# A transformer block on one core: a fifth adding transfer in attention, loads in pieces, scores behind the products

## The chip, the cores and the metric

The kernel runs on one core of a Trainium2 chip. The metric is the device time of one execution in microseconds, as the median of several runs. Its engines work side by side, each through its own queue of instructions: TensorE (PE; its weight loads are shown as PEld), VectorE (DVE), ScalarE (ACT), GpSimd (POOL) and SyncE (SP), which here only issues DMA transfers. GpSimd issues DMA transfers of its own, some of which add what they read to what lies at their destination.

## What is computed

The reference is a transformer block over 4 sequences of 2048 tokens with 512 channels: a layer norm, then attention with 16 heads of 32 channels beside a feed-forward part (two chosen experts), and the sum with the input. The change touches attention alone:

```python
attn = jnp.einsum('bhqd,bhkd->bhqk', q, k) * scale
attn = jax.nn.softmax(attn, axis=-1)
out = jnp.einsum('bhqk,bhkd->bhqd', attn, v)
```

## The kernel before

The program has three stages: `dense_stage` (layer norm, queries, keys, values, experts), `attention_stage` and `output_stage`. Only the middle one is changed. It goes through 16 items (a sequence and four of its heads), two to a turn, and through four groups of 512 queries in each item: 64 groups `g`. Keys and queries are held as high and low parts stacked on 96 partitions (`k_x`, `q_x`), with one more row that subtracts the row's maximum.

**Two passes.** For each group TensorE computes the scores twice. *Units* (64 to a group, `mx_ps`) serve the maxima: VectorE reduces each to `unit_max`, and at the end of a group's units a small transpose and ScalarE turn the maxima into `shift`, which SyncE loads into row 96 of the next group's `q_x`. *Scores* (64 to a group, `st_ps`, keys on the partitions) go to ScalarE, which writes their exponentials to `p_sb`, a ring of seven slots. *Products* multiply the exponentials by the values into `o_ps`.

**The order on TensorE** is written out by hand in `STEPS` (line 653): eight strings, one for each step of a group, in which U is a unit of a later group, S a score, V the 16 instructions of products, T the transpose, and Z the matmuls of a sum. A unit, a sum and the transpose each take the next of four banks `mx_ps` and wait until VectorE has read what was in it; a score takes one of three banks `st_ps`.

**The sums of the exponentials.** GpSimd adds the two slots of each pair of key blocks (`pair`, line 832) into one of four slots `p_pair`, named a, b, c, d in a group; eight pair adds to a group. Four adding transfers (`join`, line 839) gather them: a<-b, a<-c, d<-b, d<-c. After the eighth pair add, a ninth add of GpSimd puts b on a (line 874). TensorE sums over the partitions with a matrix of ones (`sums`, line 1017), in three parts listed in `PARTS` (line 603): the part after two transfers in step 7, the part after four transfers in step 2 of the next group, the part after the ninth add in step 3 of the next group. VectorE gathers the three in `sum_raw`.

**The inverse.** SyncE moves the sums into a compact tile (`spread_sums`), VectorE inverts them in step 5 (`invert`), SyncE stores the inverse to DRAM, waits for that store, and reads it back onto all partitions with four transfers (`spread_inverse`, line 750). GpSimd multiplies with it (`normalise`, line 826), in `group` (line 842) ahead of the eighth pair add. ScalarE copies the products out of `o_ps` (`copy_o`, line 889) once the products are done and the normalising of the group before is.

**SyncE's queue** is in order (`turn`, from line 778). At the start of each group it issues the loads of the next item: in the first group keys of two heads, in the next two groups one head each, in the fourth the values, and with each the three parts of a set of queries; then the sums, the shift, the inverse's store and spread, and the store of the group's result.

Of the kernel before, what the change touches and what calls it, by code (L numbers as in the profile page):

```python
# [15 lines left out]
F32 = mybir.dt.float32  # L16
F32R = mybir.dt.float32r
U32 = mybir.dt.uint32
ALU = mybir.AluOpType
# [5 lines left out]
H, D = 16, 32  # L25
# [4 lines left out]
TOK = 512  # L30
# [3 lines left out]
NQ = B * HQ  # L34
KT = N // P
# [540 lines left out]
def attention_stage(nc, qh_d, ql_d, kh_d, kl_d, v_d, inv_d, o_d):  # L576
# [25 lines left out]
    NA, NJ = NP + 1, 4  # L602
    PARTS = [(2, 0, False, 7), (4, 0, True, 10), (0, NA, False, 11)]
    NS = len(PARTS)
    ctx = ExitStack()
    with ctx:
# [3 lines left out]
        def sem(name):  # L610
# [42 lines left out]
        STEPS = ["USUSUSUVUSSUSUSUS", "USUSUSUVUSSUSUSUS", "USUSUSUVZUSSUSUSUS", "USUSUSUVZUSSUSUSUS",  # L653
                 "USUSUSUVUSSUSUSUS", "USUSUSUVUSSUSUSUS", "USUSUSUVTUSSUSUSUS", "USUSUSUVZUSSUSUSUS"]
# [67 lines left out]
        with nc.Block() as block:  # L722

            @block.sync
            def _(sp):
                def load_keys(it, u, heads):
                    for part, src in enumerate((kh_d, kh_d, kl_d)):
                        sp.dma_start(k_x[u][part * D:(part + 1) * D, heads, :].bitcast(F32),
                                     src[it, heads.start * D:heads.stop * D, :].rearrange("(h d) n -> d h n", d=D)).then_inc(k_ld[u], 16)

                def load_values(it, u):
                    sp.dma_start(v_sb[u][:, :, :], v_d[it, :, :, :]).then_inc(v_ld[u], 16)

                def load_queries(it, qc):
                    for part, src in enumerate((qh_d, ql_d, qh_d)):
                        sp.dma_start(q_x[qc][part * D:(part + 1) * D, :, :].bitcast(F32),
                                     src[it, :, qc * TOK:(qc + 1) * TOK].rearrange("(h d) n -> d h n", d=D)).then_inc(q_ld[qc], 16)
# [11 lines left out]

                def spread_inverse(count):  # L750

                    sp.wait_ge(inv_done, count)
                    sp.dma_start(inv_d.rearrange("h (r n) -> (h r) n", n=QR), inv_t[:, :]).then_inc(inv_st, 16)
                    sp.wait_ge(inv_st, count * 16)
# [18 lines left out]
                load_values(0, 0)  # L773
                load_shift(1, 0)

                def turn(L, first, last):
                    for g in range(G):
                        u, qc = g // QC, g % QC
                        it, more = L * 2 + u, not (last and u == 1)
                        if qc == 0 and more:  # L780

                            sp.wait_ge(pv_done, L * G * KT + g * KT)
                            load_keys(it + 1, 1 - u, slice(0, 2))
                        if qc > 0 and more:

                            sp.wait_ge(st_ready, L * G * SK + g * SK)
                            if qc < 3:
                                load_keys(it + 1, 1 - u, slice(qc + 1, qc + 2))
                            else:
                                load_values(it + 1, 1 - u)  # L790
                            load_queries(it + 1, qc - 1)
                        if qc == 0 and not (first and u == 0):
                            sp.wait_ge(st_ready, L * G * SK + g * SK)
                            load_queries(it, QC - 1)
# [12 lines left out]
                spread_sums(ALL_READS + len(PARTS_AT) - PARTS_IN)  # L807
                spread_inverse(NQ * QC)
# [4 lines left out]
            def _(pool):  # L813
# [28 lines left out]
                def group(at):  # L842
                    a, b, c, d = pair_slots(at)
                    if at > 0:
                        pool.wait_ge(joined, at * NJ * 16)
                    pair(at, 0, a)
                    pool.wait_ge(pair_done, at * NA)
# [16 lines left out]
                    pair(at, 5, c)  # L864
                    pool.wait_ge(sum_done, at * NS + 1)
# [125 lines left out]
            def _(pe):  # L991
# [56 lines left out]
                def turn(L, first, last):  # L1048
                    for g in range(G):
                        u, qc = g // QC, g % QC  # L1050

                        def next_unit(j, i):
# [5 lines left out]
                            if n == 0:  # L1058
# [3 lines left out]
                                if (g + ahead) // QC > 0 or not first:  # L1062
                                    pe.wait_ge(k_ld[nu], (L + (g + ahead) // G + nu) * 144)
# [12 lines left out]
                        def products(j):  # L1076
# [6 lines left out]
                            if j == 1:  # L1083
                                pe.wait_ge(v_ld[u], (L + 1) * 16)
# [223 lines left out]
```

## Time and profile before

| | us |
|---|---|
| median of three runs | 4837.95 (4837.81 to 4843.53) |
| the profiled execution, its own time | 4836.55 |
| its span, first to last instruction | 4834.7 |

| engine | busy us | share of the span | instructions |
|---|---|---|---|
| TensorE | 4691.4 | 97% | 24396 |
| TensorE's weight loads | 2773.0 | 57% | 24396 |
| VectorE | 3170.4 | 66% | 5296 |
| ScalarE | 2398.9 | 50% | 4653 |
| GpSimd | 3223.0 | 67% | 1117 |

The shares are averages over three stages. Attention fills about two thirds of the span, from some 1320 to 4640 us, and there GpSimd is busy for 90% or more. A row of a timeline gives the start, the duration and the instruction; instructions of one kind that follow one another are merged, with their count, and the bracket at the end tells how long the engine was idle before and what ended that. Matmuls are pipelined, so the distance between two starts tells more than a duration. SyncE's rows are the issues of transfers, not the transfers.

### The profile page before, as it was taken

The page shows a single profiled execution, that of the slowest core. Times are in us where ns is not written, and L with a number is a line of the kernel's source. Part 1 is how long each engine was busy: PE and PEld are TensorE (multiplying, and loading weights), DVE is VectorE, ACT ScalarE, POOL GpSimd, SP SyncE. Part 2 cuts the span into 40 slices and gives each one's busy share as a digit, 9 for nine tenths or more (in the row PEclk, how much of TensorE's full clock was granted, in tenths as well). Part 3 has the DMA queues.
Part 4 walks back from the last instruction along what each step waited for, and adds up shares of the span by engine and source line. Part 5 has one row for each costly group of instructions (what it writes and reads, how often), then busy time and mean ns, then how long its engine had stood idle before and what let it go on. Part 6 is the DMA issues. An engine that isn't in the chain of part 4 may idle for free. (4 is left out here: it accounts for less than half of the span.)

```text
span 4834.7 us, 66456 instructions
## 1 busy us (share of the span) xinstructions
PE 4691.4 (97%) x24396; PEld 2773.0 (57%) x24396; DVE 3170.4 (66%) x5296; ACT 2398.9 (50%) x4653; POOL 3223.0 (67%) x1117
## 2 busy tenths in 40 slices
PE   8999999999899999999999999999999999999979
PEld 6887878878654444444444444444444444444447
DVE  4223232333188888888888888888888888888534
ACT  2111121121146666666666666666666666666621
POOL 1121212121249998989989989999899998998920
PEclk9999999999979999999999999999999999999989
DMA  5344343343346655656656566665665656655466
GB/s 172 103 127 122 109 138 102 119 129 111 91 106 130 137 127 125 138 125 137 133 124 139 124 131 136 126 139 120 132 137 124 140 125 132 137 124 121 90 225 236
DMA packets 254215, 633.49 MB, mean 131 GB/s; under 512 B 45252, under 2 KB 79044, under 8 KB 212936
## 3 DMA queue, kind: packets, MB, share of 16 engines
q0 software_dynamic: 36864, 268.45, 27.8%
q1 hardware_dynamic: 217032, 360.85, 27.0%
q8 instruction: 193, 3.16, 0.3%
q14 instruction: 126, 1.03, 0.1%
HBM read 224.96 MB, written 134.74 MB: 74 GB/s over the span
## 5 line engine op out<-in xcount | busy, mean ns | idle before, releaser
L927 DVE TENSOR_REDUCE unit_max<-mx_ps 128x1 f32<-128x512 f32 x4096 | 2535.2, 681 | 317.0 <-PE mx_ps L1002 310.9
L836 POOL TENSOR_TENSOR p_pair<-p_sb 128x2048 f32<-128x2048 f32 x512 | 2439.8, 4811 | 185.3 <-PE mx_ps L1026 128.3
L913 ACT ACTIVATE p_sb<-st_ps 128x512 f32<-128x512 f32 x4096 | 2061.9, 628 | 905.5 <-PE st_ps L1073 905.5
L1002 PE MATMUL mx_ps<-k_x,q_x 96*128 96x512 f32 x4096 | 1684.9, 415 | 21.5 <-DMA k_x<-k_lo_d 19.6
L1073 PE MATMUL st_ps<-q_x,k_x 97*128 97x512 f32 x4096 | 1607.8, 413 | 37.9 <-ACT p_sb L913 37.3
L1073 PEld LDWEIGHTS st_ps<-q_x,k_x 97*128 97x128 f32 x4096 | 770.3, 188 | 599.3 <-ACT p_sb L913 512.8
L1002 PEld LDWEIGHTS mx_ps<-k_x,q_x 96*128 96x128 f32 x4096 | 784.6, 192 | 456.7 <-DVE unit_max L927 234.3
L1014 PE MATMUL o_ps<-p_sb,v_sb 128*32 128x512 f32 x8192 | 986.8, 599 | 0.0
L285 POOL TENSOR_TENSOR h_lo<-h_f,h_hi 128x512 fp32r<-128x512 f32 x128 | 165.2, 1291 | 687.7 <-DVE h_hi L469 687.7
L1014 PEld LDWEIGHTS o_ps<-p_sb,v_sb 128*32 128x32 f32 x8192 | 214.0, 109 | 494.1 <-ACT p_sb L913 309.8
L469 DVE CAST h_hi<-h_f 128x512 fp32r<-128x512 f32 x128 | 55.0, 431 | 541.9 <-ACT h_f L342 541.9
L342 ACT ACTIVATE h_f<-rot,b_sb 128x512 f32<-128x512 f32 x128 | 88.2, 689 | 642.3 <-PE rot L505 642.3
L840 POOL DMA_DIRECT2D p_pair<-p_pair x256 | 244.2, 954 | 159.9 <-DMA p_pair<-p_pair 134.4
L874 POOL TENSOR_TENSOR p_pair<-p_pair 128x2048 f32<-128x2048 f32 x64 | 293.5, 4586 | 5.0
L326 ACT ACTIVATE qk_hi<-rot,qk_bias 128x512 fp32r<-128x512 f32 x128 | 88.2, 689 | 384.2 <-DMA q_lo_d<-qk_lo 176.3
L944 DVE TENSOR_TENSOR sum_raw<-mx_ps,sum_raw 128x512 f32<-128x512 f32 x128 | 88.5, 691 | 207.4 <-PE mx_ps L1026 207.4
L503 PE MATMUL rot<-xnT_hi,wq_hi 128*128 128x512 f32 x512 | 201.8, 394 | 18.1 <-DVE qk_lo L433 9.9
L503 PE MATMUL acc<-we_hi,h_hi 128*128 128x512 f32 x512 | 205.5, 401 | 6.0 <-POOL h_lo L285 4.4
L1026 PE MATMUL mx_ps<-p_pair,ones 128*32 128x512 f32 x1536 | 201.7, 597 | 9.8 <-DMA p_pair<-p_pair 7.8
L268 POOL TENSOR_TENSOR rstd<-var_eps,minus_half 128x4 f32<-128x4 f32 (+1 forms) x17 | 16.9, 992 | 287.4 <-DVE var_eps L372 287.4
L433 DVE SCALAR_TENSOR_TENSOR qk_lo<-rot,qk_bias,qk_hi 128x512 fp32r<-128x512 f32 x128 | 95.7, 748 | 164.8 <-ACT qk_hi L326 164.4
L503 PE MATMUL rot<-xnT_hi,we_hi 128*128 128x512 f32 x512 | 200.0, 391 | 1.9 <-DVE v_out L455 1.9
(94 smaller groups left out, 3926.8 us busy)
## 6 DMA issues: line engine op xcount, KB each, us to landing
p_pair<-p_pair POOLq DMA_DIRECT2D x256, 1024.0 KB, 7.3
q_x<-q_hi_d SPq DMA_DIRECT2D x128, 256.0 KB, 8.6
k_x<-k_hi_d SPq DMA_DIRECT2D x68, 256.0 KB, 7.3
xt<-x SPq DMA_DIRECT2D x64, 256.0 KB, 2.7
stage<-w SPq DMA_DIRECT2D x32, 512.0 KB, 5.1
q_hi_d<-qk_hi SPq DMA_DIRECT2D x64, 256.0 KB, 3.0
q_lo_d<-qk_lo SPq DMA_DIRECT2D x64, 256.0 KB, 3.9
k_hi_d<-qk_hi SPq DMA_DIRECT2D x64, 256.0 KB, 2.6
```

The costliest lines, as they stand in the source:

```text
L285: pool.tensor_tensor(h_lo[:, n % 2, :], h_f[:, n % 2, :], h_hi[:, n % 2, :].bitcast(F32), ALU.subtract).then_inc(h_lo_done, 1)
L433: dve.scalar_tensor_tensor(out=qk_lo[:, m % 2, :], in0=rot[m % 4][:, :], scalar=qk_bias[:, m:m + 1], in1=qk_hi[:, m % 2, :].bitcast(F32), ...
L503: pe.matmul(out, lh, rh, start=start and k == 0, stop=False)
L836: pool.tensor_tensor(p_pair[:, slot, :, :], p_sb[:, n % SLOTS, :, :], p_sb[:, (n + 1) % SLOTS, :, :], ALU.add).then_inc(pair_done, 1)
L840: pool.dma_start(p_pair[:, into, :, :], p_pair[:, slot, :, :], accum_op=ALU.add).then_inc(joined, 16)
L874: pool.tensor_tensor(p_pair[:, a, :, :], p_pair[:, a, :, :], p_pair[:, b, :, :], ALU.add).then_inc(pair_done, 1)
L913: act.activation(p_sb[:, (L * G * KT + n) % SLOTS, h, :], st_ps[bank(g, m)][:, :], ACT.Exp, scale=SCALE).then_inc(exp_done, 1)
L927: dve.reduce_max(unit_max[:, n // 4, n % 4:n % 4 + 1], mx_ps[UNIT_PLACE[n] % RING][:, :], AX.X).then_inc(bank_read, 1)
L1002: pe.matmul(mx_ps[UNIT_PLACE[n] % RING][:, :], q_x[qc][0:R, h, t * P:(t + 1) * P], k_x[u][0:R, h, kc * 512:(kc + 1) * 512], start=True, st ...
L1014: op = pe.matmul(o_ps[rows, :], v_sb[u][:, kt, rows], p_sb[:, (L * G * KT + n) % SLOTS, h, :], start=(kt == 0), stop=(kt == KT - 1))
L1026: op = pe.matmul(mx_ps[place % RING][h * D:(h + 1) * D, :], ones[:, :], p_pair[:, slot, h, :], start=True, stop=True)
L1073: pe.matmul(st_ps[bank(g, m)][:, :], k_x[u][:, h, kt * P:(kt + 1) * P], q_x[qc][:, h, :], start=True, stop=True).then_inc(st_ready, 1)
```

## The change

It does six things in the attention stage.

- The ninth add of GpSimd becomes a fifth adding transfer, a<-b, which waits for the eighth pair add and for the fourth transfer. The last part of the sums now waits for five transfers (`NA`, `NJ`, `PARTS`).
- At the start of a group the first pair add waits for four transfers of the group before, the second one for all five.
- `normalise` moves from behind the fourth transfer to ahead of the wait before the seventh pair add.
- The loads of keys and values are cut into four pieces to a group, of 256 KB each, and those of the queries into three. They wait for scores of the group: two pieces for the 10th, two for the 16th, two query parts for the 33rd, one for the 57th, and stand on SyncE's queue between the other transfers.
- The store of the inverse is issued ahead of the load of the shift instead of behind it.
- In `STEPS`, two scores instead of a unit follow the products (or the sum or transpose behind them), and two units come together later in the step.

GpSimd's order, one group, from its first two pair adds on. Before (L836 is a pair add, L840 a transfer, L830 normalising, L874 the ninth add):

```order
L836 TENSOR_TENSOR p_pair<-p_sb 128x2048 x2
L840 DMA p_pair<-p_pair 128x2048
L836 TENSOR_TENSOR p_pair<-p_sb 128x2048 x2
L840 DMA p_pair<-p_pair 128x2048
L836 TENSOR_TENSOR p_pair<-p_sb 128x2048
L840 DMA p_pair<-p_pair 128x2048
L836 TENSOR_TENSOR p_pair<-p_sb 128x2048 x2
L840 DMA p_pair<-p_pair 128x2048
L830 TENSOR_TENSOR o_inv<-o_raw,o_inv 128x512
L836 TENSOR_TENSOR p_pair<-p_sb 128x2048
L874 TENSOR_TENSOR p_pair<-p_pair 128x2048
```

Now (L855 a pair add, L859 a transfer, L849 normalising):

```order
L855 TENSOR_TENSOR p_pair<-p_sb 128x2048 x2
L859 DMA p_pair<-p_pair 128x2048
L855 TENSOR_TENSOR p_pair<-p_sb 128x2048 x2
L859 DMA p_pair<-p_pair 128x2048
L855 TENSOR_TENSOR p_pair<-p_sb 128x2048
L859 DMA p_pair<-p_pair 128x2048
L855 TENSOR_TENSOR p_pair<-p_sb 128x2048
L849 TENSOR_TENSOR o_inv<-o_raw,o_inv 128x512
L855 TENSOR_TENSOR p_pair<-p_sb 128x2048
L859 DMA p_pair<-p_pair 128x2048
L855 TENSOR_TENSOR p_pair<-p_sb 128x2048
L859 DMA p_pair<-p_pair 128x2048
```

Normalising stands one pair add and one transfer earlier, and the last row is a transfer.

SyncE's order, one group with keys of one head. Before:

```order
L728 DMA k_x<-k_hi_d 32x2048 x2
L728 DMA k_x<-k_lo_d 32x2048
L736 DMA q_x<-q_hi_d 32x4x512
L736 DMA q_x<-q_lo_d 32x4x512
L736 DMA q_x<-q_hi_d 32x4x512
L748 DMA sum_t<-sum_raw 128x1x16
L742 DMA q_x<-shift 1x16x128
L753 DMA inv_d<-inv_t 128x16
L758 DMA o_inv<-inv_d 32x512 x4
L764 DMA o_d<-o_inv 128x512
```

Now, the group with the pieces of two heads:

```order
L727 DMA k_x<-k_lo_d 32x2048
L727 DMA k_x<-k_hi_d 32x2048 x2
L727 DMA k_x<-k_lo_d 32x2048
L752 DMA sum_t<-sum_raw 128x1x16
L736 DMA q_x<-q_hi_d 32x4x512
L736 DMA q_x<-q_lo_d 32x4x512
L756 DMA inv_d<-inv_t 128x16
L746 DMA q_x<-shift 1x16x128
L764 DMA o_inv<-inv_d 32x512 x4
L736 DMA q_x<-q_hi_d 32x4x512
L770 DMA o_d<-o_inv 128x512
```

Four pieces of keys stand ahead of the sums, two parts of the queries behind them, the inverse ahead of the shift, and the last part of the queries behind the spread of the inverse.

TensorE's order around the products of a plain step (mx_ps is a unit, st_ps a score, o_ps the products). Before:

```order
L1014 MATMUL o_ps<-p_sb,v_sb 32x512 x8
L1002 MATMUL mx_ps<-k_x,q_x 128x512
L1073 MATMUL st_ps<-q_x,k_x 128x512 x2
L1002 MATMUL mx_ps<-k_x,q_x 128x512
L1073 MATMUL st_ps<-q_x,k_x 128x512
L1002 MATMUL mx_ps<-k_x,q_x 128x512
L1073 MATMUL st_ps<-q_x,k_x 128x512
L1002 MATMUL mx_ps<-k_x,q_x 128x512
```

Now:

```order
L1035 MATMUL o_ps<-p_sb,v_sb 32x512 x8
L1094 MATMUL st_ps<-q_x,k_x 128x512 x2
L1023 MATMUL mx_ps<-k_x,q_x 128x512
L1094 MATMUL st_ps<-q_x,k_x 128x512
L1023 MATMUL mx_ps<-k_x,q_x 128x512 x2
L1094 MATMUL st_ps<-q_x,k_x 128x512
L1023 MATMUL mx_ps<-k_x,q_x 128x512
L1094 MATMUL st_ps<-q_x,k_x 128x512
```

Behind the products stand two scores where a unit and two scores stood; two units come together three rows later.

The diff, cut to its core:

```diff
-    NA, NJ = NP + 1, 4
-    PARTS = [(2, 0, False, 7), (4, 0, True, 10), (0, NA, False, 11)]
+    NA, NJ = NP, 5
+    PARTS = [(2, 0, False, 7), (4, 0, True, 10), (5, 0, False, 11)]
...
-        STEPS = ["USUSUSUVUSSUSUSUS", "USUSUSUVUSSUSUSUS", "USUSUSUVZUSSUSUSUS", "USUSUSUVZUSSUSUSUS",
-                 "USUSUSUVUSSUSUSUS", "USUSUSUVUSSUSUSUS", "USUSUSUVTUSSUSUSUS", "USUSUSUVZUSSUSUSUS"]
+        STEPS = ["USUSUSUVSSUSUUSUS", "USUSUSUVSSUSUUSUS", "USUSUSUVZSSUSUUSUS", "USUSUSUVZSSUSUUSUS",
+                 "USUSUSUVSSUSUUSUS", "USUSUSUVSSUSUUSUS", "USUSUSUVTSSUSUUSUS", "USUSUSUVZSSUSUUSUS"]
...
-                        if qc == 0 and more:
-
-                            sp.wait_ge(pv_done, L * G * KT + g * KT)
-                            load_keys(it + 1, 1 - u, slice(0, 2))
...
+                        def load(part, score):
+
+                            if part < 4 and more:
+                                sp.wait_ge(st_ready, L * G * SK + g * SK + score)
+                                if qc < 3:
+                                    load_keys(it + 1, 1 - u, (4 * qc + part) // 3, (4 * qc + part) % 3)
+                                else:
+                                    load_values(it + 1, 1 - u, part)
...
+                        load(0, 10)
+                        load(1, 10)
+                        load(2, 16)
+                        load(3, 16)
                         if not (first and g == 0):
                             spread_sums(read_count(L, g, PART_PLACE[LAST_PART], first, last))
+                        load(4, 33)
+                        load(5, 33)
+                        if not (first and g == 0):
+                            store_inverse(L * G + g)
                         if not (last and g == G - 1):
                             load_shift(L * G + g + 2, (qc + 1) % QC)
                         if not (first and g == 0):
                             spread_inverse(L * G + g)
+                        load(6, 57)
+                        if not (first and g == 0):
                             store_group(L, it - 1 if qc == 0 else it, (qc - 1) % QC, L * G + g)
...
                     if at > 0:
+                        pool.wait_ge(joined, (at * NJ - 1) * 16)
+                    pair(at, 0, a)
+                    if at > 0:
                         pool.wait_ge(joined, at * NJ * 16)
-                    pair(at, 0, a)
-                    pool.wait_ge(pair_done, at * NA)
                     pair(at, 1, b)
...
                     pair(at, 5, c)
+                    if at > 0:
+                        normalise(at)
                     pool.wait_ge(sum_done, at * NS + 1)
                     pair(at, 6, a)
                     pool.wait_ge(pair_done, at * NA + 6)
                     pool.wait_ge(joined, (at * NJ + 3) * 16)
                     join(d, c)
-                    if at > 0:
-                        normalise(at)
                     pair(at, 7, b)
                     pool.wait_ge(pair_done, at * NA + NP)
-                    pool.tensor_tensor(p_pair[:, a, :, :], p_pair[:, a, :, :], p_pair[:, b, :, :], ALU.add).then_inc(pair_done, 1)
+                    pool.wait_ge(joined, (at * NJ + 4) * 16)
+                    join(a, b)
```

## Rows read from the trace of the kernel before

**Rows 1.** TensorE's timeline, one group: start, us, line, instruction, count, [idle <-releaser]

```profile
3003.04 1.92 PE L1014 MATMUL o_ps<-p_sb,v_sb 128*32 128x512 f32 x16
...
3008.95 1.92 PE L1014 MATMUL o_ps<-p_sb,v_sb 128*32 128x512 f32 x16
...
3012.00 0.63 PE L1073 MATMUL st_ps<-q_x,k_x 97*128 97x512 f32 x2
...
3013.16 0.43 PE L1073 MATMUL st_ps<-q_x,k_x 97*128 97x512 f32 x1
...
3015.39 0.40 PE L1002 MATMUL mx_ps<-k_x,q_x 96*128 96x512 f32 x1
3015.72 1.92 PE L1014 MATMUL o_ps<-p_sb,v_sb 128*32 128x512 f32 x16
...
3046.97 1.92 PE L1014 MATMUL o_ps<-p_sb,v_sb 128*32 128x512 f32 x16
...
3051.04 0.50 PE L1073 MATMUL st_ps<-q_x,k_x 97*128 97x512 f32 x1 [0.55 <-ACT p_sb L913]
...
3053.65 1.92 PE L1014 MATMUL o_ps<-p_sb,v_sb 128*32 128x512 f32 x16
```

**Rows 2.** Waits, 56 groups: engine, line <- releaser: us in total, times, longest

```profile
ACT o_raw L893 <- POOL o_inv L830: 122.7, 56, 2.5
POOL p_pair L840 <- DMA p_pair<-p_pair: 119.0, 56, 2.7
```

**Rows 3.** GpSimd's timeline, the same group

```profile
3008.35 9.13 POOL L836 TENSOR_TENSOR p_pair<-p_sb 128x2048 f32<-128x2048 f32 x2
3017.78 0.89 POOL L840 DMA_DIRECT2D p_pair<-p_pair  x1 [0.30 <-POOL p_pair L836]
...
3027.50 1.19 POOL L840 DMA_DIRECT2D p_pair<-p_pair  x1
...
3035.27 0.88 POOL L840 DMA_DIRECT2D p_pair<-p_pair  x1 [1.96 <-DMA p_pair<-p_pair]
...
3043.08 4.62 POOL L836 TENSOR_TENSOR p_pair<-p_sb 128x2048 f32<-128x2048 f32 x1 [2.28 <-PE mx_ps L1026]
3047.64 0.86 POOL L840 DMA_DIRECT2D p_pair<-p_pair  x1
3048.26 1.55 POOL L830 TENSOR_TENSOR o_inv<-o_raw,o_inv 128x512 f32<-128x512 f32 x1
3049.49 4.86 POOL L836 TENSOR_TENSOR p_pair<-p_sb 128x2048 f32<-128x2048 f32 x1
3054.43 4.59 POOL L874 TENSOR_TENSOR p_pair<-p_pair 128x2048 f32<-128x2048 f32 x1
```

**Rows 4.** Stretches: us, busy by engine, then PEclk, DMA share, GB/s

```profile
3048.90:3054.10 5.20, 4.65 (x20) 2.63 (x24) 4.26 (x7) 4.20 (x9) 5.20 (x2) 1.00 1.03 202
3108.00:3108.50 0.50, 0.50 (x4) 0.30 (x2) 0.50 (x2) 0.50 (x2) 0.50 (x1) 1.00 1.11 246
3157.50:3158.00 0.50, 0.50 (x4) 0.41 (x3) 0.50 (x1) 0.42 (x1) 0.50 (x1) 1.00 1.02 426
```

**Rows 5.** The page's DMA issues: count, KB each, median us to landing

```profile
p_pair<-p_pair POOLq DMA_DIRECT2D x256, 1024.0 KB, 7.3
```

**Rows 6.** DMA queues that moved bytes, 3050.30 to 3053.00 us: packets, MB, share

```profile
q0 software_dynamic: 80, 0.66, 120.1%
```

**Rows 7.** SyncE's timeline of DMA issues, start of the stage and the same group

```profile
1425.38 0.79 SPq L728 DMA_DIRECT2D k_x<-k_hi_d  x2
...
3050.23 2.51 SPq L728 DMA_DIRECT2D k_x<-k_hi_d  x2
```

**Rows 8.** GpSimd's timeline at the start of the stage

```profile
1427.67 0.88 POOL L840 DMA_DIRECT2D p_pair<-p_pair  x1
...
1439.78 4.59 POOL L836 TENSOR_TENSOR p_pair<-p_sb 128x2048 f32<-128x2048 f32 x1 [1.91 <-DMA p_pair<-p_pair]
```

**Rows 9.** Waits of SyncE's DMA queue, 56 groups

```profile
SPq L758 <- DMA inv_d<-inv_t: 253.5, 56, 6.6
```

More of the change, by code:

```diff
@@ L725, in _, with load_keys, load_values, load_query_part @@
             def _(sp):
[L726 to L732, printed above, removed]
+                def load_keys(it, u, h, part):
+                    sp.dma_start(k_x[u][part * D:(part + 1) * D, h, :].bitcast(F32),
+                                 (kh_d, kh_d, kl_d)[part][it, h * D:(h + 1) * D, :]).then_inc(k_ld[u], 16)
+                def load_values(it, u, quarter):
+                    kts = slice(quarter * KT // 4, (quarter + 1) * KT // 4)
+                    sp.dma_start(v_sb[u][:, kts, :], v_d[it, :, kts, :]).then_inc(v_ld[u], 16)
+                def load_query_part(it, qc, part):
+                    src = (qh_d, ql_d, qh_d)[part]
+                    sp.dma_start(q_x[qc][part * D:(part + 1) * D, :, :].bitcast(F32),
+                                 src[it, :, qc * TOK:(qc + 1) * TOK].rearrange("(h d) n -> d h n", d=D)).then_inc(q_ld[qc], 16)
                 def load_queries(it, qc):
-                    for part, src in enumerate((qh_d, ql_d, qh_d)):
-                        sp.dma_start(q_x[qc][part * D:(part + 1) * D, :, :].bitcast(F32),
-                                     src[it, :, qc * TOK:(qc + 1) * TOK].rearrange("(h d) n -> d h n", d=D)).then_inc(q_ld[qc], 16)
+                    for part in range(3):
+                        load_query_part(it, qc, part)
                 def load_shift(count, qc):
@@ L772, in _ @@
                     load_queries(0, qc)
-                load_values(0, 0)
+                for quarter in range(4):
+                    load_values(0, 0, quarter)
                 load_shift(1, 0)
@@ L779, in turn @@
                         it, more = L * 2 + u, not (last and u == 1)
-                        if qc == 0 and more:
-                            sp.wait_ge(pv_done, L * G * KT + g * KT)
-                            load_keys(it + 1, 1 - u, slice(0, 2))
[L784 to L794, printed above, removed]
+                        def load(part, score):
[5 more added lines that the diff above has]
+                                    load_values(it + 1, 1 - u, part)
+                            if part >= 4 and qc > 0 and more:
+                                sp.wait_ge(st_ready, L * G * SK + g * SK + score)
+                                load_query_part(it + 1, qc - 1, part - 4)
+                            if part >= 4 and qc == 0 and not (first and u == 0):
+                                sp.wait_ge(st_ready, L * G * SK + g * SK + score)
+                                load_query_part(it, QC - 1, part - 4)
+                        load(0, 10)
+                        load(1, 10)
+                        load(2, 16)
+                        load(3, 16)
                         if not (first and g == 0):
                             spread_sums(read_count(L, g, PART_PLACE[LAST_PART], first, last))
+                        load(4, 33)
+                        load(5, 33)
+                        if not (first and g == 0):
+                            store_inverse(L * G + g)
                         if not (last and g == G - 1):
@@ L807, in _ @@
                 spread_sums(ALL_READS + len(PARTS_AT) - PARTS_IN)
+                store_inverse(NQ * QC)
                 spread_inverse(NQ * QC)
@@ L1062, in next_unit @@
                                 if (g + ahead) // QC > 0 or not first:
-                                    pe.wait_ge(k_ld[nu], (L + (g + ahead) // G + nu) * 144)
+                                    pe.wait_ge(k_ld[nu], (L + (g + ahead) // G + nu) * 192)
                             emptied(L, g, PLACE[j, i], first, last)
@@ L1083, in products @@
                             if j == 1:
[L1084 removed]
+                                pe.wait_ge(v_ld[u], (L + 1) * 64)
                                 if not (first and g == 0):
```

3 lines of the change are left out of this document (2 added, 1 removed).

## The prediction

> **What bounds the kernel now.** I read the timelines engine by engine over one group of 512 queries in the middle of the attention stage, because one period repeats there. The products of the second step start at 3003.04 us and again at 3053.65: a group takes 50.61 us [rows 1], and there are 64 of them. In the TensorE timeline the reader should see that the queue hardly ever stops. A plain step takes 3008.95 - 3003.04 = 5.91 us, a step with a sum behind its products 3015.72 - 3008.95 = 6.77, and the step over the group's border 3053.65 - 3046.97 = 6.68, where one stall of 0.55 is marked [rows 1]. Inside a step the 16 matmuls of units and scores run in two paces. From 3012.00 to 3013.16 five follow one another in 1.16 us, 0.232 each; the nine up to 3015.39 take 2.23, 0.248 each: from there ScalarE's exponentials set the pace. So some 9 x 0.016 = 0.14 us of a step are lost to the order of scores and units.
>
> The list of waits gives the border's stall: ScalarE's copy of the products waits for GpSimd's normalising, 122.7 us in 56 groups, 2.2 each, and GpSimd waits 119.0 / 56 = 2.13 us a group for an adding transfer [rows 2]. GpSimd's timeline shows why it is late [rows 3]: eight pair adds of 4.6 to 4.9 us, four issues of a transfer, the normalising at 3048.26, the ninth add (4.59). It idles 2.28 us at 3043.08 until TensorE has read a slot, so GpSimd is close to the bound but is not it. The clock is granted in full (1.00) here [rows 4].
>
> **TensorE's part of the change.** Three edits help TensorE. Two scores straight behind the products start ScalarE one unit (0.23 us) earlier in each step, so its 8 exponentials no longer hold back the second half: 8 x 0.14 = 1.1 us a group. Normalising ahead of the seventh pair add takes it off the border: it comes before the wait that ends at 3043.08 instead of behind a pair add and an issue, about 5 us earlier than the 3048.26 of now, so ScalarE's copy no longer waits; the border step falls from 6.68 to a plain 5.91, 0.77 us. The moved units cost nothing: a ring of four banks covers them, and with that cover gone one bank wait of a few tenths would return. TensorE alone would then need 50.61 - 1.1 - 0.8 = **48.7 us a group**.
>
> **GpSimd's part: a chain of three transfers.** The ninth add goes (4.59 us of GpSimd) and a transfer comes. That frees the engine but not the path, since the new transfer a<-b has to wait for the fourth (into the same data), the second pair add of the next group has to wait for the new one, and the third transfer already waits for the second. I add up the loop from one second pair add to the next [rows 3]:
> - second pair add (starts 3008.35 + 4.57 = 3012.92) to the first transfer at 3017.78: 4.86
> - to the second transfer at 3027.50 (two pair adds beside the first transfer): 9.72
> - to the third: 7.77 in this group with 1.96 of it idle; the mean idle is 2.13 [rows 2], so 7.94
> - the third transfer's issue and the sixth pair add, 3035.27 to 3043.08 less 2.28 idle: 5.53
> - normalising, 3049.49 - 3048.26: 1.23; seventh pair add, 3047.64 - 3043.08: 4.56
> - fourth transfer to the fifth, as from second to third: 7.9
> - fifth transfer until it has landed: 7.3 [rows 5], and 0.1 to start the add
>
> The sum is **49.1 us** if nothing comes between. Everything else on GpSimd (eighth and first pair add, 4.9 each) fits inside the 7.9 of a transfer. So the loop is already 0.4 us longer than TensorE's 48.7: GpSimd falls behind until the last sum (the one that reads the fifth transfer) holds TensorE up. The slots of the exponentials do not: each pair add still ends some 3 us before its slots are wanted.
>
> **What the loads do to it.** Loads and adding transfers share the 16 DMA engines. From 3050.30 to 3053.00 only the transfers' queue moves bytes, although two loads were issued from 3050.23 on: they come behind the transfer issued first [rows 6, 7]. The reverse stands at the start of the stage: six loads issued from 1425.38 on (the row holds the first two), a transfer at 1427.67, and the add that waits for it starts at 1439.78 [rows 7, 8]. It landed after 12.0 us instead of 7.3. First issued is first served, both ways. The Trainium skill ("DMA: Bandwidth & Descriptors", section Queues, rings and completion order) says that each DMA engine takes turns between its queues, packet by packet; the trace does not agree, as no packet of the loads' queue moved in those 2.7 us. By the skill's rule the loads would cost the chain their full time; that is the second rival below, and the sum here goes by the rows.
>
> A transfer moves its data in 5.2 us [rows 4], so between two chained ones the engines stand free for 7.9 - 5.2 = 2.7. The change issues four load pieces of 256 KB in just this place. Where the last sum holds TensorE, the fifth transfer was issued 7.4 us before that sum and the fourth 15.3. The pieces behind the 16th score are issued 4.2 us after the second step's products (1.9 for those, 8 starts of 0.232, 0.4 for the score), and the sum would run 5.8 + 6.6 + 1.8 us after the same point: 10.0 us ahead of it, 2.6 ahead of the fifth transfer. Those behind the 10th score come 4.8 us earlier still, about when the fourth is issued. So four pieces share one gap of 2.7 us. Price of a key piece: at 246 GB/s [rows 4] 1.07 us, four 4.3, so 1.6 too much; by the start of the stage (4.7 late plus the 2.3 that they had led, over six) 1.17 and up to 1.22 with their earlier first byte, four 4.9, so 2.2 too much. I take 1.9. Of values, at 426 GB/s 0.62 each [rows 4], four 2.5: they fit, 0 to 0.4, I take 0.2. Three groups in four load keys, one values: (3 x 51.0 + 49.3) / 4 = **50.6 us**, with ends 50.3 and 50.85. That is the period of now.
>
> The other pieces cost nothing: two query pieces delay the first transfer by at most 2.4 us, of which 9.72 - 7.9 = 1.8 is slack, and 0.6 at worst stays in the upper end; the third has 11.3 - 7.9 = 3.4 us to spare. The early inverse: now the store is issued behind the third transfer, and SyncE waits for it 253.5 us in 56 groups, 4.5 each [rows 9]. Issued at the fifth step's inversion it lands before the third transfer, and the four spreads go out right behind the shift. Were they behind that transfer, normalising would wait some 3 us once and the next transfer would come behind the spreads.
>
> **Sum.** Some 57 steady groups x (50.6 - 50.61) = 0 (ends -18 and +14). The last four groups load no keys: 4 x -1.5 = -6. The first two or three run at TensorE's pace until GpSimd is behind: -4. At the end the fifth transfer takes 7.9 where the add took 4.6: +3.3. Together about -6 us. The profiled execution took 4836.55 us (span 4834.7), so 4830; the median of the runs is 1.4 above it, and I forecast **4832 us**, own range 4805 to 4855. A measurement of this kernel can tell about 0.2% (10 us) from no change.
>
> **Rivals.**
> 1. *TensorE keeps the lead.* If the pieces do fall into separate gaps, two behind the fourth and two behind the fifth transfer, the loop is 49.1: (49.1 - 50.61) x 60 + 3 = -88, 4750; with transfers somewhat quicker than 7.9, TensorE's 48.7 holds: -112, 4726. For it: 2.7 us do hold two pieces of 1.1. Against it: that needs the fifth transfer issued before the 16th score, and a loop longer than TensorE's moves it past that. Chance 0.2.
> 2. *The loads cost the chain more than what is left of the gap* (slower). If the engines share, a transfer lasts longer by what is loaded beside it and the gap no longer absorbs it: key groups 49.1 + 4.3 = 53.4, value groups 51.6, mean 52.9: +2.3 x 57 = +130, 4965. With half of that overlap: +1.1 x 57, 4900. The point that decides: more than 2.7 + 1.5 us of loading added per group to the fourth and fifth transfer. For it: in the 12.0 us landing some of the price was mixing. Against it: rows 6. Chance 0.3, most of it near the lower end, 4860 to 4900.
> 3. The forecast itself, the transfers' chain in place of the add: chance 0.5.
>
> **Chances.** Faster by over 0.2% (below 4828): all of rival 1 and 0.2 from the forecast's lower half, 0.4. Within 0.2%: 0.22. Slower: rival 2 and 0.08 of the forecast, 0.38. For 8 in 10 the range reaches from 4745 (leaves out the faster half of rival 1) to 4895.
>
> **What would show it.** Right: TensorE's idle time moves to the last sum, waiting for a transfer, 1 to 2 us a group; GpSimd idles at two transfers' issues and before the second pair add; ScalarE's copy waits no more; the fourth or fifth transfer lands after 9 us or more in key groups and near 7.3 in value groups. Wrong: no wait of TensorE for transfers and plain steps near 5.8 (rival 1); loads' packets moving while a transfer is under way, with landings of 9 to 11 us in every group (rival 2); or plain steps still at 5.9 us, which would undo the first term.

## The result: 1.6% slower

The changed kernel takes **4914.56 us** (median of four runs, 4907.76 to 4922.33) against 4838.32 in the same job: a ratio of 1.0156, 95% interval 1.0138 to 1.0173. The forecast was 4832, in a range of 4745 to 4895: the time is 20 us above the range, and the sign is that of the second rival.

From the page of the profile after: the span, the engines' busy times, and the adding transfers (count, KB each, median us from issue to landing).

```profile
span 4914.1 us, 66612 instructions
...
PE 4684.6 (95%) x24396; PEld 2969.9 (60%) x24396; DVE 3156.3 (64%) x5296; ACT 2401.6 (49%) x4653; POOL 2990.8 (61%) x1117
...
p_pair<-p_pair POOLq DMA_DIRECT2D x320, 1024.0 KB, 8.3
```

GpSimd lost the 64 ninth adds (3223.0 us busy before, 2990.8 now), which gave nothing, and half the transfers now take 8.3 us or more, where the median was 7.3 [rows 5]. GpSimd's timeline after, one group of the steady part (L855 a pair add, L859 a transfer, L849 normalising), answers to [rows 3]:

```profile
2998.38 4.57 POOL L855 TENSOR_TENSOR p_pair<-p_sb 128x2048 f32<-128x2048 f32 x1 [1.57 <-DMA p_pair<-p_pair]
3003.25 0.88 POOL L859 DMA_DIRECT2D p_pair<-p_pair  x1 [0.30 <-POOL p_pair L855]
...
3012.97 1.15 POOL L859 DMA_DIRECT2D p_pair<-p_pair  x1
...
3020.71 0.88 POOL L859 DMA_DIRECT2D p_pair<-p_pair  x1 [1.95 <-DMA p_pair<-p_pair]
...
3028.89 1.30 POOL L849 TENSOR_TENSOR o_inv<-o_raw,o_inv 128x512 f32<-128x512 f32 x1 [2.70 <-DMA o_inv<-inv_d]
3030.14 4.59 POOL L855 TENSOR_TENSOR p_pair<-p_sb 128x2048 f32<-128x2048 f32 x1
3034.65 0.89 POOL L859 DMA_DIRECT2D p_pair<-p_pair  x1
3035.27 4.89 POOL L855 TENSOR_TENSOR p_pair<-p_sb 128x2048 f32<-128x2048 f32 x1
3044.14 0.89 POOL L859 DMA_DIRECT2D p_pair<-p_pair  x1 [3.98 <-DMA p_pair<-p_pair]
...
3051.18 4.61 POOL L855 TENSOR_TENSOR p_pair<-p_sb 128x2048 f32<-128x2048 f32 x1 [1.51 <-DMA p_pair<-p_pair]
3056.09 0.88 POOL L859 DMA_DIRECT2D p_pair<-p_pair  x1 [0.30 <-ACT p_sb L934]
```

The five transfers are issued at 3003.25, 3012.97, 3020.71, 3034.65 and 3044.14, the next group's first at 3056.09. Between the fourth and the fifth lie 9.49 us, and GpSimd stands idle for 3.98 of them. (The wait of 2.70 us for the inverse makes the way from the third to the fourth 13.94 us here; four of the 55 groups averaged below are like that, the others take some 10.95.) SyncE's timeline (issues of loads) tells what was beside the fourth; it answers to [rows 7]:

```profile
3004.56 0.33 SPq L736 DMA_DIRECT2D q_x<-q_hi_d  x1
...
3035.37 0.78 SPq L727 DMA_DIRECT2D k_x<-k_hi_d  x2
3040.27 0.31 SPq L727 DMA_DIRECT2D k_x<-k_lo_d  x1
3040.62 1.02 SPq L727 DMA_DIRECT2D k_x<-k_hi_d  x1
```

All four pieces of keys are issued while the fourth transfer is under way, none beside the fifth. The DMA queues that moved bytes from 3037 to 3038 us (q0 carries GpSimd's transfers, q1 SyncE's; packets, MB, share), where [rows 6] show q0 alone:

```profile
q0 software_dynamic: 16, 0.13, 62.8%
q1 hardware_dynamic: 16, 0.13, 34.8%
```

Sixteen packets each: the engines take turns. That transfer landed after 9.0 us, the fifth after 7.0. The waits after, over 56 groups, answer to [rows 2]:

```profile
POOL p_pair L859 <- DMA p_pair<-p_pair: 385.4, 113, 7.3
...
POOL p_pair L855 <- DMA p_pair<-p_pair: 104.6, 57, 3.0
PE mx_ps L1047 <- DMA p_pair<-p_pair: 103.5, 86, 3.8
...
ACT o_raw L914 <- POOL o_inv L849: 10.0, 6, 1.7
```

The border's wait is gone (10.0 us where it was 122.7), and TensorE has a new one of the same size: a sum waits for a transfer, 103.5 / 56 = 1.85 us a group. TensorE's timeline has both kinds, first a sum that waited for a fourth transfer, then one that waited for a fifth:

```profile
2990.95 1.07 PE L1047 MATMUL mx_ps<-p_pair,ones 128*32 128x512 f32 x8 [2.73 <-DMA p_pair<-p_pair]
...
3051.24 1.07 PE L1047 MATMUL mx_ps<-p_pair,ones 128*32 128x512 f32 x8 [0.60 <-DMA p_pair<-p_pair]
```

Each of these sums starts 0.14 us after a landing, which tells them apart: 41 of the 86 waits, 61.9 us, are for the fourth transfer, 45 waits, 41.6 us, for the fifth.

The first of the two rows has a sequel. Two stretches behind it (us, busy by engine, then PEclk, DMA share, GB/s, as in [rows 4]):

```profile
2992.00:2998.83 6.83, 6.83 (x19) 5.07 (x16) 5.25 (x8) 4.16 (x8) 5.26 (x3) 0.50 0.76 154
2998.83:3003.25 4.42, 4.42 (x32) 1.97 (x32) 2.12 (x4) 1.54 (x4) 4.12 (x1) 1.00 0.00 0
```

TensorE's granted clock falls to 0.50 (1.2 GHz in place of 2.4). That happens nine times in the 55 groups averaged below, for 3.4 or 6.8 us, each time beside a stop of 1.9 to 3.8 us at a sum. It happens in no such group of the kernel before, nor of the runs below in which the loads are left out or wait for the fifth transfer. The four groups with the late inverse stand each right behind a group with such a fall. The 46 groups without one average 51.64 us, so most of the loss is there without the clock.

I also averaged the distances between issues on GpSimd's timeline over 55 groups, the 5th to the 59th, and the landings over 32, the 17th to the 48th. T1 to T5 are the transfers of a group.

| us | T1 to T2 | T2 to T3 | T3 to T4 | T4 to T5 | T5 to T1 | a group |
|---|---|---|---|---|---|---|
| forecast, loads included | 9.72 | 7.94 | 11.32 | 9.38 | 12.26 | 50.6 |
| changed kernel | 9.92 | 8.30 | 11.17 | 10.24 | 12.29 | 51.92 |
| without later keys and values | 10.16 | 8.22 | 10.97 | 8.17 | 12.26 | 49.77 |
| pieces five scores later | 9.93 | 8.18 | 11.62 | 8.40 | 13.63 | 51.77 |
| pieces behind T5's landing | 10.53 | 8.22 | 10.95 | 8.13 | 12.28 | 50.11 |
| the same, one query part moved | 9.76 | 8.27 | 11.25 | 8.16 | 12.22 | 49.66 |

| landing, us | T1 | T2 | T3 | T4 | T5 |
|---|---|---|---|---|---|
| before | 7.2 | 7.4 | 7.4 | 7.5 | - |
| changed kernel | 9.1 | 7.8 | 8.2 | 9.8 | 7.3 |
| pieces five scores later | 9.1 | 7.8 | 8.3 | 7.9 | 8.6 |
| pieces behind T5's landing | 9.9 | 7.8 | 7.9 | 7.7 | 7.3 |
| the same, one query part moved | 8.2 | 7.8 | 9.7 | 7.7 | 7.2 |

57 groups x (51.92 - 50.6) = 75 of the 83 us that the forecast missed.

### The profile page after: what moved, and what is told of

Same layout as the page of the kernel before. It is cut to its first block and busy times, and to the rows that moved or that the text cites. A ratio compares the mean times of both kernels' runs of the same rounds, so it can differ in the third digit from the quotient of the medians.

```text
span 4914.1 us, 66612 instructions
## 1 busy us (share of the span) xinstructions
PE 4684.6 (95%) x24396; PEld 2969.9 (60%) x24396; DVE 3156.3 (64%) x5296; ACT 2401.6 (49%) x4653; POOL 2990.8 (61%) x1117
## 5 line engine op out<-in xcount | busy, mean ns | idle before, releaser
L948 DVE TENSOR_REDUCE unit_max<-mx_ps 128x1 f32<-128x512 f32 x4096 | 2506.1, 681 | 334.6 <-PE mx_ps L1023 332.0
L855 POOL TENSOR_TENSOR p_pair<-p_sb 128x2048 f32<-128x2048 f32 x512 | 2490.5, 4905 | 177.6 <-DMA p_pair<-p_pair 116.8
L1023 PE MATMUL mx_ps<-k_x,q_x 96*128 96x512 f32 x4096 | 1582.9, 410 | 21.8 <-DMA k_x<-k_lo_d 19.9
L1094 PEld LDWEIGHTS st_ps<-q_x,k_x 97*128 97x128 f32 x4096 | 742.0, 191 | 544.2 <-issue 379.9
L859 POOL DMA_DIRECT2D p_pair<-p_pair x320 | 314.4, 982 | 466.2 <-DMA p_pair<-p_pair 427.8
L1047 PEld LDWEIGHTS mx_ps<-p_pair,ones 128*32 128x32 f32 x1536 | 42.3, 109 | 275.2 <-issue 163.6
L504 PE MATMUL rot<-xnT_lo,wq_hi 128*128 128x512 f32 x512 | 201.2, 393 | 0.0
L505 PE MATMUL rot<-xnT_hi,wq_lo 128*128 128x512 f32 x512 | 201.1, 393 | 0.0
```

Source lines behind the costliest of these rows:

```text
L504: pe.matmul(out, lh, rl, start=False, stop=False)
L505: op = pe.matmul(out, ll, rh, start=False, stop=stop and k == len(pairs) - 1)
L855: pool.tensor_tensor(p_pair[:, slot, :, :], p_sb[:, n % SLOTS, :, :], p_sb[:, (n + 1) % SLOTS, :, :], ALU.add).then_inc(pair_done, 1)
L859: pool.dma_start(p_pair[:, into, :, :], p_pair[:, slot, :, :], accum_op=ALU.add).then_inc(joined, 16)
L948: dve.reduce_max(unit_max[:, n // 4, n % 4:n % 4 + 1], mx_ps[UNIT_PLACE[n] % RING][:, :], AX.X).then_inc(bank_read, 1)
L1023: pe.matmul(mx_ps[UNIT_PLACE[n] % RING][:, :], q_x[qc][0:R, h, t * P:(t + 1) * P], k_x[u][0:R, h, kc * 512:(kc + 1) * 512], start=True, st ...
```

## The experiments

Each ratio is to the kernel before, run in the same job. **What bounds the changed kernel: its loop of transfers, or the order on TensorE?** The old `STEPS` in the changed kernel:

```diff
-        STEPS = ["USUSUSUVSSUSUUSUS", ...
+        STEPS = ["USUSUSUVUSSUSUSUS", ...
```

> The changed kernel with the order of scores and units of before. Theory A (the loop of adding transfers sets the period, 51.9 us a group, and the load pieces lengthen the fourth transfer by 2.3 us): TensorE alone would need 48.7 + 1.1 = 49.8 us, still less than 51.9, so nothing changes: 4900 to 4930 us. Rival B (TensorE's new order is what costs): back towards the kernel before, 4840 to 4870.

4920.14 us, 1.0157 (1.014 to 1.0173): the order is worth nothing here, so TensorE doesn't bound it.

**Are the loads the price?** Keys and values from the third item on are not loaded:

```diff
-                            if part < 4 and more:
+                            if part < 4 and first and u == 0:
...
```

> The changed kernel without the pieces of keys and values after the second item (the items from the third on are computed with the keys and values of the first two; queries are still loaded). Theory A: the fourth transfer lands after 7.3 to 7.5 us instead of 9.7, the loop falls by 2.3 to 2.6 us a group to about 49.5: 4750 to 4790 us. Rival B: no change, above 4890. Rival C (the fifth transfer costs by itself, loads or not): 4840 to 4890.

4803.57 us, 0.9919 (0.9902 to 0.9935). The loads, with all that follows from them, cost 111 us of the changed kernel; T4 to T5 falls from 10.24 to 8.17. It is still 13 us above what was expected: the loop takes 49.77 us a group where I had 49.5, with 10.16 from T1 to T2, where the query parts still are.

**The same loads in another place.** SyncE waits for the fifth transfer ahead of the pieces:

```diff
                                 sp.wait_ge(st_ready, L * G * SK + g * SK + score)
+                                if part == 0 and not (first and g == 0):
+                                    sp.wait_ge(joined, (L * G + g) * NJ * 16)
```

> The changed kernel with one more wait on SyncE: the four pieces of keys or values of a group go out once the fifth transfer of the group before has landed, when no transfer runs until the first one, 4.9 us later. Theory A: four key pieces take 4.3 us there and the first transfer has 1.8 us of slack; the fourth lands after 7.5, the loop is 49.5 to 50.3: 4770 to 4820 us. If pieces and query parts together push the first transfer past its slack, up to 4850. Rival C: no better than 4890.

4807.27 us, 0.9922 (0.9905 to 0.9939), within 4 us of the run with no such loads. Between the fifth transfer's landing and the next group's first transfer lies a pair add, and no transfer of the chain is under way.

**Parts of the change on the kernel before.** The new order alone, and the new order with the early normalising and the early inverse:

```diff
+        STEPS = ["USUSUSUVSSUSUUSUS", ...
```

> The kernel before with TensorE's new order alone. Theory A: plain steps fall from 5.91 to the 5.83 us that the changed kernel shows, 0.6 us a group, but normalising still stands behind the seventh pair add, so ScalarE's copy waits a little longer at the border: 4805 to 4830 us beside 4840. If the group's loads (now nearer to the fourth transfer) lengthen it: 4840 to 4870. Rival B (the order itself costs): above 4850.

```diff
                     pair(at, 5, c)
+                    if at > 0:
+                        normalise(at)
...
                     join(d, c)
-                    if at > 0:
-                        normalise(at)
```

> The kernel before (ninth add on GpSimd, four transfers, loads at the group's start) with only the new order on TensorE, normalising ahead of the seventh pair add, and the early store of the inverse. Theory A: no loop of three transfers, so TensorE's 48.7 to 49.0 us a group holds: 4730 to 4765 us. If GpSimd's own work (48.3 us a group without its wait for TensorE) and its waits are the bound: 4765 to 4800. Rival B: 4838 or slower.

The order alone: 4813.57 us, 0.994 (0.9923 to 0.9956), as expected. With the early normalising and the early inverse: **4948.29**, 1.0209 (1.0192 to 1.0226), 183 us above theory A and in rival B's range. GpSimd's timeline of this kernel (L843 a transfer, L833 normalising, L839 a pair add):

```profile
3059.40 1.28 POOL L833 TENSOR_TENSOR o_inv<-o_raw,o_inv 128x512 f32<-128x512 f32 x1 [3.37 <-DMA o_inv<-inv_d]
...
3065.17 0.89 POOL L843 DMA_DIRECT2D p_pair<-p_pair  x1
...
3078.70 9.06 POOL L839 TENSOR_TENSOR p_pair<-p_sb 128x2048 f32<-128x2048 f32 x2 [3.36 <-DMA p_pair<-p_pair]
```

And its SyncE:

```profile
3060.71 0.36 SPq L765 DMA_DIRECT2D o_d<-o_inv  x1
3063.27 1.49 SPq L728 DMA_DIRECT2D k_x<-k_hi_d  x2
```

SyncE's queue is in order: the store of the result waits for normalising, and the loads stand behind the store. With normalising early the loads go out 1.90 us ahead of the fourth transfer; before, they went out 2.59 behind it (3050.23 - 3047.64 [rows 3, 7]). The transfer now lands 13.5 us after its issue (11.9 in the mean of the groups). The late normalising of the kernel before had been holding the loads in a harmless place. But the early one also has a price of its own: it waits for the inverse (3.37 us above, 122.0 us in 43 waits between 1700 and 4600 us), whose spreads go out behind the third transfer. T3 to T4 takes 13.58 us where it is 11.66 with the order alone, T4 to the next T1 21.23 where it is 20.82. No run tells how much of the loss is the loads' and how much that wait's.

**The ninth add in the changed kernel**, in place of the fifth transfer:

```diff
...
-                    pool.wait_ge(joined, (at * NJ + 4) * 16)
-                    join(a, b)
+                    pool.tensor_tensor(p_pair[:, a, :, :], p_pair[:, a, :, :], p_pair[:, b, :, :], ALU.add).then_inc(pair_done, 1)
```

> The changed kernel with GpSimd's ninth add in place of the fifth transfer; the load pieces stay where they are. Theory A: the fourth transfer still lands after 9 to 10 us, but nothing is chained to it before the next group's first pair add, 11.3 us after its issue; TensorE's own pace of 49.4 us a group (as without loads) holds: 4765 to 4800 us. If the fourth transfer's length reaches TensorE through the sum that reads it, or the inverse is late: 4800 to 4840. Rival D (the pieces cost by themselves, whatever stands in place of the add): above 4870.

4819.94 us, 0.9943 (0.9924 to 0.9963): the second branch, groups of 50.0 to 51.1, with normalising waiting for the inverse (67.1 us in 22 groups). T4 still lands after 9.4 us in the mean, but the kernel is 95 us faster than with the fifth transfer: pieces and fifth transfer cost this much only together, as the run without the pieces shows from the other side.

**The query parts later**, behind the inverse's store, on top of the pieces behind the fifth:

```diff
-                        load(4, 33)
-                        load(5, 33)
                         if not (first and g == 0):
                             store_inverse(L * G + g)
+                        load(4, 33)
+                        load(5, 33)
```

> The pieces behind the fifth transfer as in e3_loads_behind_fifth, and the two query parts of the 33rd score moved behind the store of the inverse, off the first transfer. Theory A: from first to second transfer 9.72 us again instead of 10.2 to 10.8, the loop 49.5: 4780 to 4800 us, TensorE's pace. Rival: the query parts now meet the second transfer, which is chained: 8.5 us or more from second to third and 4800 to 4830.

4812.35 us, 0.9938 (0.9922 to 0.9955): T1 to T2 falls to 9.70, T2 to T3 rises to 9.0. The price moved to the next transfer.

**The store ahead of the pieces**, as in the kernel before:

```diff
+                        if not (first and g < 2):
+                            sp.wait_ge(st_ready, L * G * SK + g * SK + 10)
+                            store_group(L, L * 2 + (g - 2) // QC, (g - 2) % QC, L * G + g - 1)
                         load(0, 10)
...
                         load(6, 57)
-                        if not (first and g == 0):
-                            store_group(L, it - 1 if qc == 0 else it, (qc - 1) % QC, L * G + g)
```

> The changed kernel with the store of a group's result held back to the next group's 10th score, just ahead of the first two pieces on SyncE's queue, as it stood ahead of the loads in the kernel before. Theory E (a store that waits behind a running transfer holds up what is queued behind it, so that the loads keep off the transfer): the fourth transfer lands after 7.3 to 8 us, the fifth is pushed back by four pieces and the store, 50.5 to 51.5 us a group: 4860 to 4910 us. Theory F (loads share the engines with a running transfer whatever stands ahead of them): the fourth lands after 10 us or more and the store's 256 KB come on top, 4920 to 4990 us.

5003.89 us, 1.0322 (1.0304 to 1.034), slower than either theory: groups of 52.3 to 54.2 by the kind of load. T4 lands after 9.8 us in the mean, as in the changed kernel; T5 after 8.3, where it was 7.3. T4 was spared only where the store came late: in six groups it went out 1.6 us or more behind T4, and in five of them T4 landed in 7.6 to 8.1 us.

**Does a load that comes late take nothing from a transfer?** Twenty transfers alone, behind the attention stage, each with two loads at a set offset (two of them with none), one trial for each:

```diff
+                    pool.tensor_tensor(p_pair[:, 2, 0, 0:64], ...).then_inc(probe_go, 1)
+                    join(0, 1)
...
+                    sp.wait_ge(probe_at, t + 1)
+                    sp.dma_start(k_x[0][0:D, i, :].bitcast(F32), kh_d[0, i * D:(i + 1) * D, :])
```

> The changed kernel, and after its attention stage 20 adding transfers of 1 MB one at a time, each with two 256 KB loads issued at a set offset: none, some 2 and 1 us before the transfer, with it, and some 0.5 to 6 us after it; first with key pieces, then with value pieces. The span grows by some 300 us, which tell nothing. What is read is how long each transfer takes to land. Theory S (the engines always take turns between the two queues): every load issued within the first 5 us lengthens the transfer by about what it moves, 2 us for two key pieces and 1.2 for two value pieces: 9.3 and 8.5 against 7.3 alone, at all offsets from -1 to +3. Theory O (a load issued soon after the transfer, or before it, takes turns; one issued more than some 1.3 us after it comes behind the whole transfer): 9 us and more up to an offset of about +1, and 7.3 to 7.6 from about +1.5 on, with the loads landing only some 7 us after the transfer's issue. Theory Q, the prediction's (first issued is first served): 7.3 at every offset from 0 on.

| first load behind the transfer, us | none | -1.8 | -0.85 | 0.3 | 0.6 to 0.7 | 1.2 to 1.4 | 1.7 | 2.3 | 3.4 | 4.5 |
|---|---|---|---|---|---|---|---|---|---|---|
| landing beside two key pieces | 7.0 | 7.0 | 8.0 | 9.2 | 8.7 | 9.3 | 9.0 | 9.3 | 8.2 | 7.4 |
| beside two value pieces | 6.9 | 7.2 | 8.2 | 9.0 | 8.1 | 8.1 | 8.1 | 7.9 | 7.8 (7.9 at 3.1) | - |

GpSimd's timeline for the keys at 1.4, with the start of the next trial; then SyncE's:

```profile
4764.72 0.87 POOL L876 DMA_DIRECT2D p_pair<-p_pair  x1
4775.29 0.31 POOL L926 TENSOR_TENSOR p_pair<-p_pair 128x64 f32<-128x64 f32 x1 [9.71 <-DMA k_x<-k_hi_d]
```

```profile
4766.13 1.57 SPq L840 DMA_DIRECT2D k_x<-k_hi_d  x2
```

The queues that moved bytes from 4766.50 to 4770.00 us, and then from 4770.70 to 4773.00:

```profile
q0 software_dynamic: 80, 0.66, 100.3%
...
q1 hardware_dynamic: 64, 0.39, 57.7%
q0 software_dynamic: 32, 0.13, 33.6%
```

For 3.5 us the transfer's queue moves bytes alone, the very picture of [rows 6], and the transfer still lands after 9.3 us. Of its 144 packets 128 carry 8 KB and 16 are small (under 512 bytes); the last 32, 16 of each kind (0.13 MB), go through beside 64 packets of the keys. Theory O and the prediction's theory Q fall. The price is theory S's for keys from 0.3 to 2.3 us, 0.9 to 2.1 us for values; but the turns at all times that theory S rests on are not what these 3.5 us show.

**The same in the kernel**, the pieces five scores later:

```diff
-                        load(0, 10)
-                        load(1, 10)
-                        load(2, 16)
-                        load(3, 16)
+                        load(0, 15)
+                        load(1, 15)
+                        load(2, 21)
+                        load(3, 21)
```

> The changed kernel with its four load pieces five scores (some 4 us) later: two behind the 15th score and two behind the 21st, so the first two fall some 2.5 to 4.5 us behind the fourth transfer's issue, and the last two about at the fifth's. Theory S, sharing (a piece costs the transfer it overlaps, up to an offset of some 3.5 us, as the isolated transfers showed for keys): two pieces' worth goes from the fourth transfer to the fifth, the sum of both stays, 4890 to 4930 us, with the fourth landing after 8 to 9 us and the fifth after 8.5 to 9.5. Theory O (more than 1.5 us behind, a load takes nothing from the transfer): the fourth lands in 7.4 to 7.6, only the fifth is late, by 1 to 2 us; 4825 to 4865 us.

4912.42 us, 1.0146 (1.0129 to 1.0163): theory S's time, but not by its sum. T4 lands in 7.9 where it was 9.8 (7.7 without later keys and values), T5 in 8.6 where it was 7.3. The way from T4 to the next T1 is 0.50 us shorter than in the changed kernel; T3 to T4 gives 0.45 back. For in 10 of the 55 groups T3 to T4 takes 12.6 to 16.0 us, as normalising is late, each time right behind a group in which TensorE's granted clock fell to 0.50. So pieces that come this late cost T4 itself little here, and T5 1.3 of the 1.9 us that T4 is spared. That the time is the same has another reason, most likely the fallen clock, which no run sets apart.

**A version faster than both.** Pieces behind the fifth transfer's landing, and one query part moved from the first transfer to the third, which has some 3 us to spare:

```diff
+                                if part == 0 and not (first and g == 0):
+                                    sp.wait_ge(joined, (L * G + g) * NJ * 16)
...
                         load(4, 33)
-                        load(5, 33)
...
+                        load(5, 57)
                         load(6, 57)
```

> The changed kernel with the four pieces behind the fifth transfer's landing (as in the run with loads behind the fifth), and besides one of the two query pieces of the first transfer moved behind the third, which has some 3 us to spare. Theory S: the first transfer loses some 0.5 us of its lengthening, the third's slack takes the piece; groups 49.6 to 49.9 us in place of 50.1, 4785 to 4800 us. Rival: what still binds is TensorE's own pace of 49.4 and the border, not the first transfer: 4800 to 4812, as with both pieces there.

**4787.46 us**, 0.9886 (0.9869 to 0.9902). T1 lands in 8.2 where it was 9.9, T3 in 9.7 where it was 7.9, and T3 to T4 grows by only 0.3. GpSimd's timeline of this kernel shows the empty place (L861 a transfer, L857 a pair add), and SyncE's the pieces in it:

```profile
3033.96 0.88 POOL L861 DMA_DIRECT2D p_pair<-p_pair  x1 [2.03 <-ACT p_sb L936]
...
3040.99 4.58 POOL L857 TENSOR_TENSOR p_pair<-p_sb 128x2048 f32<-128x2048 f32 x1 [1.54 <-DMA p_pair<-p_pair]
3045.87 0.88 POOL L861 DMA_DIRECT2D p_pair<-p_pair  x1 [0.30 <-ACT p_sb L936]
```

```profile
3040.99 0.32 SPq L727 DMA_DIRECT2D k_x<-k_hi_d  x1
3041.35 0.42 SPq L727 DMA_DIRECT2D k_x<-k_lo_d  x1
3041.82 0.88 SPq L727 DMA_DIRECT2D k_x<-k_hi_d  x2
```

TensorE's timeline of the same kernel (L1037 the products of a step, L1049 a sum) shows what binds now:

```profile
2991.36 1.92 PE L1037 MATMUL o_ps<-p_sb,v_sb 128*32 128x512 f32 x16
...
2998.04 1.92 PE L1037 MATMUL o_ps<-p_sb,v_sb 128*32 128x512 f32 x16
3003.86 1.92 PE L1037 MATMUL o_ps<-p_sb,v_sb 128*32 128x512 f32 x16
...
3040.54 1.92 PE L1037 MATMUL o_ps<-p_sb,v_sb 128*32 128x512 f32 x16
```

A group in 49.18 us without a wait: 5.82 for a plain step, 6.68 for a step with a sum, five and three of them. The mean group is 49.66, so the loop still adds some 0.5.

## Why the prediction was wrong

**The step that failed** is "First issued is first served, both ways", and with it that a piece beside a chained transfer costs only what does not fit into the gap of 2.7 us. Rows 6 were read as a rule of order. They show that the loads' packets had not begun, and that transfer did land on time, after 7.3 us; they do not show that a transfer loses nothing to a load issued behind it. Alone on the chip, the same picture goes with a landing 2.3 us late. And in the changed kernel the first pieces go out between 1.0 us ahead of T4 and 1.7 behind it (in 54 of 55 groups; 0.7 behind in the group above), the queues alternate from early on, and T4 lands after 9.8 us where it was 7.5. The Trainium skill ("DMA: Bandwidth & Descriptors", section Queues, rings and completion order) says that the engines take turns between queues; the trace of the changed kernel agrees, 16 packets of each in 1 us. The 2.7 us of [rows 6] and the 3.5 us of the transfer alone, with one queue moving bytes, do not.

**The term that was mis-sized** is the loads' on T4 to T5: priced at 1.9 for keys and 0.2 for values above 7.9. Measured over the groups, T4 to T5 is 10.39 beside keys and 9.80 beside values; in the same groups without later keys and values it is 8.19 and 8.07. So the loads cost 2.2 and 1.7: 2.07 in the mean where 1.48 was forecast, 0.59 too little, and the bare distance was put 0.27 too low. T1 to T2 adds 0.20, beside the query parts that the prediction had cost nothing (9.70 with them moved). T2 to T3 adds 0.36, and does so nearly as much with the other loads out of the way (8.22 to 8.27); what lengthens it stays open. T3 to T4 gives back 0.15. Together with 0.03 more from T5 to T1, that is 1.31 us a group. The place of the pieces was as forecast, two about at T4's issue and two some 5 us behind it. The sign for the value groups was not: T4 lands after 9.3 us beside values and 9.9 beside keys, rival 2's 9 us or more, not near 7.3.

**Put at nothing**: what a stop of TensorE brings with it. The prediction found the clock granted in full and left it so. The stops at the sums took it to 0.50 nine times, and with those groups the mean is 51.92 where it is 51.64 without them.

**Half of rival 2's price.** Its full form (53.4 and 51.6 us) was too high, as T4 to T5 has a part of the gap left; its half form, 4900, is 15 us under the result. The point it named, more than 2.7 + 1.5 us of loading added to the fourth and fifth transfer, does not describe what happened: value pieces by the forecast's own price come to 2.5, and cost 1.7.

**TensorE alone** was put at 48.7 us a group; it is 49.2. The border's 0.77 came as forecast: no wait there in the changed kernel, and the border step is a plain one. The order gives 0.08 to 0.09 a step (5.91 to 5.82), not 0.14. For the change this decided nothing, since the loop binds.

**What was right**: the loop of transfers, not TensorE, sets the group's time; the idle time of TensorE moved to sums that wait for a transfer, 1 to 2 us a group (1.85), though only 0.74 of it to the last one, the rest to the one before, which waits for T4; GpSimd's freed 4.6 us are worth nothing; normalising leaves the border; the loop without loads (49.1 forecast, 49.77 with queries only).

## What to carry to other kernels

Where transfers wait for one another, a load placed beside one of them costs the chain much of its own duration (2.2 of 4.3 us for four key pieces, 1.7 of 2.5 for values), even if its bytes appear to come last. Look in the chain for the stretch in which no transfer is under way, or for a transfer with slack, and bind the loads to that (here a wait for the fifth transfer's landing): the same loads then cost 4 us in place of 111. And before moving a step early, ask what stands behind it on its in-order queues: early normalising, with the early inverse, cost the kernel before 2%, as it let the loads go and waited for the inverse besides.

## What the runs showed that I had not expected

Two key pieces (32 partitions) lengthen a transfer by up to 2.3 us, two value pieces (128 partitions) by up to 2.1 when issued at its start but by only 1.2 from 0.6 us on, though both move 512 KB. A load issued 0.3 to 0.7 us behind a transfer alternates with it from early on (its first packet comes 1.3 to 3.3 us behind the issue); one issued 1.2 us behind or later, with the transfer alone, moves no byte until most of the transfer's are through (from 6.0 to 7.3 us behind its issue) and then shares the end. What decides between the two stays open, and so does why T4 of the kernel before lands in 7.3 us with a store 2.2 and keys 2.6 us behind it, where alone, with keys 2.3 behind, it takes 9.3.
